# An attention and mixture-of-experts block on one Trainium2 core: one key tile fewer summed by matmuls in the long query blocks, and the last normalisation of a group moved from VectorE to ScalarE

## The chip, the core and the metric

The kernel runs on one core of one Trainium2 chip. The core has TensorE (PE in the rows), VectorE (DVE), ScalarE (ACT), GpSimd (POOL) and the engine that issues most DMAs (SP). Each has its own instruction queue and goes through it in order; semaphores tie the queues together. The metric is the device time of one execution in microseconds (us), and less is better. Between fast executions of one kernel it agrees within about 0.3%.

## The reference

Two sequences of 2048 tokens with 512 features go through one layer. All 16 heads have a dimension of 32 and share one key head and one value head.

```python
qkv = jnp.einsum('bsd,ed->bse', x, Wqkv_w) + Wqkv_b          # 512 for q, 32 for k, 32 for v
scores = jnp.einsum('bqhd,bkd->bhqk', q, k) * scale          # 16 heads, one k
scores = jnp.where(causal[None, None], scores, min_val)
attn = jax.nn.softmax(scores, axis=-1)
ctx = jnp.einsum('bhqk,bkd->bqhd', attn, v)
out = jnp.einsum('bsd,ed->bse', ctx, out_w) + out_b
...
x = _layernorm(x + attention(x))                             # x1
x = _layernorm(x + experts(x))                               # top 2 of 8 experts, bf16 matmuls
```

The layer normalisations have no gain and no bias: `(x - mean) / sqrt(var + 1e-5)` over the 512 features of a token.

## The kernel before, in words

A loop runs over the two sequences (`b`). In each, four **groups** `g` of 512 queries follow one another, and a group has four **blocks** `q` of 128 queries. Block `q` sees `q + 1` key tiles of 128 keys, the diagonal one first. So group 0 has 10 tiles, group 1 has 26, group 2 has 42 and group 3 has 58. `t` numbers the tiles of a sequence, `FIRST[q]` and `LAST[q]` are those of a block.

One tile goes through the engines as follows. TensorE writes its scores for all 16 heads in two halves of 1024 columns (`scores`, L1109, four matmuls of 512 columns), into a ring of three half buffers in PSUM. ScalarE takes the exponential of each half (`exp_tile`, L620) into one of six `prob` buffers. The diagonal tile is masked by GpSimd in two halves (`mask`, L492). TensorE multiplies by the values two tiles later (`times_values`, L1131, eight matmuls). A half of the ring is free again when its exponential is done: the second half of the scores of tile t + 1 waits for the first exponential of tile t.

The denominators are sums over keys. VectorE adds the `prob` buffers of a block into `psum_k` (`add`, L793, 128x2048 and both inputs in SBUF), one instruction a tile. The last `BY_PE[q]` tiles of a block are not added: in `denominators` TensorE sums them by matmuls with `ones` (L1149, eight for a tile), together with `psum_k`. `denominators(q)` comes four tiles after the block's last one, and waits for the block's last add. VectorE then inverts the sum and scales the context (L842 to L852).

After the attention tiles of a group come the output projection, the projections of the next group, x1, the router and the experts. The last piece of a group, `finish_experts(g)`, is put off on both TensorE and VectorE until the next group's attention has begun: TensorE issues the scores of the first tile and then the rest of the down projection (L1264), and VectorE adds each 128x512 result to `res`, takes mean and variance into `mv` (L866 to L870), and tells GpSimd by `mv_ready`. GpSimd makes `rstd` in two tiny instructions of 128x4 (`make_rstd`: L517 adds epsilon, L519 raises to the power -0.5). VectorE waits for that and scales four tiles of `res` (`normalise`, L876, `out_ready`). Only behind that stand its adds of the new group. The SP queue stores `res` as each tile's `out_ready` comes.

The order on each engine is the order of the code; there is no scheduler. `mv` and `rstd` exist once, and serve both normalisations of a group.

Of the kernel before, what the change touches and what calls it, by code (L numbers as in the profile page):

```python
# [35 lines left out]
P = 128  # L36
# [6 lines left out]
NG = S // BT  # L43
DC = D // P
TB = BT // P
# [16 lines left out]
LAST = [FIRST[q] + q for q in range(NQ)]  # L62
NT = len(TILES)

BY_PE = [0] + [1] * 9 + [2] * (NQ - 10)
ADDED = [t for q in range(NQ) for t in range(FIRST[q] + 1, LAST[q] + 1 - BY_PE[q])]
ADDS = len(ADDED)

# [61 lines left out]
def build(nc, xT, x, wqkvT, bq, bvk, owT, ob, rT, w1, w2, w3, out):  # L130
    ctx = ExitStack()
    with ctx:
# [51 lines left out]
        stats = sb("stats", [P, TB, 6])  # L184
        mv = sb("mv", [P, TB, 2])
        rstd = sb("rstd", [P, TB])
        rsc = sb("rsc", [P, TB, E])
        top8 = sb("top8", [P, TB, E])
        tidx = sb("tidx", [P, TB, E], U32)
# [32 lines left out]
        def half_of(t):  # L222
# [52 lines left out]
        mv_ready = sem("mv_ready")  # L275
        eps_in = sem("eps_in")
        rstd_ready = sem("rstd_ready")
        x1_ready = sem("x1_ready")
        x1_turned = sem("x1_turned")
        x1T_ready = sem("x1T_ready")  # L280
# [40 lines left out]
            xT_high: NG, xT_low: NG, part_done: NG, rpart_ready: NG,  # L321
            prod_done: E * NG,
            biased: 16 * NG, outproj: TB * NG, resid1: TB * NG, mv_ready: 2 * NG, eps_in: 2 * NG,
            rstd_ready: 2 * NG, x1_ready: TB * NG, x1_turned: TB * NG, x1T_ready: TB * NG,
            x1Tb_ready: TB * NG, routed: NG, dtop_ready: NG, etop_ready: NG, ghl_ready: NG,
            gates_turned: NG, gT_ready: NG, up_done: E * NG, gate_done: E * NG,
            silu_done: E * NG, h_done: E * NG, down_done: TB * NG, resid2: TB * NG,
# [110 lines left out]
        @block.gpsimd  # L438
        def _(pool):
            steps = [0]  # L440

            def step(ins):

                steps[0] += 1
                ins.then_inc(const_step, 1)
                pool.wait_ge(const_step, steps[0])

            nc.gpsimd.memset(rT_sb[:, :, :], 0.0).then_inc(rT_cleared, 1)
            step(nc.gpsimd.memset(ident[:, :], 0.0))
            step(nc.gpsimd.affine_select(out=ident[:, :], in_=ident[:, :], compare_op=ALU.not_equal, fill=1.0,  # L450
                                         base=0, pattern=[[-1, P]], channel_multiplier=1))
            step(nc.gpsimd.memset(pick_f, 0.0))
            for off in (0, E, 2 * E):
                step(nc.gpsimd.affine_select(out=pick_f, in_=pick_f, compare_op=ALU.not_equal,
                                             fill=1.0, base=-off, pattern=[[-1, E]],
                                             channel_multiplier=1))
            step(nc.gpsimd.memset(ident_b[:, :], 0.0))
            step(nc.gpsimd.affine_select(out=ident_b[:, :], in_=ident_b[:, :], compare_op=ALU.not_equal, fill=1.0,
                                         base=0, pattern=[[-1, P]], channel_multiplier=1))
            for e in range(E):  # L460
                step(nc.gpsimd.memset(iota8[:, e:e + 1], float(e)))
            step(nc.gpsimd.memset(ones[:, :], 1.0))
            step(nc.gpsimd.memset(ones_b[:, :], 1.0))

            step(nc.gpsimd.memset(head_pick[:, :], 1.0))
            step(nc.gpsimd.affine_select(out=head_pick[:, :], in_=head_pick[:, :], compare_op=ALU.is_ge, fill=0.0,
                                         base=0, pattern=[[-HD, HC]], channel_multiplier=1))
            step(nc.gpsimd.affine_select(out=head_pick[:, :], in_=head_pick[:, :], compare_op=ALU.is_ge, fill=0.0,
                                         base=HD - 1, pattern=[[HD, HC]], channel_multiplier=-1))
            step(nc.gpsimd.memset(causal_min[:, :], 3e38))  # L470
            step(nc.gpsimd.affine_select(out=causal_min[:, :], in_=causal_min[:, :], compare_op=ALU.is_ge,
                                         fill=-3e38, base=0, pattern=[[-1, P]], channel_multiplier=1))
            step(nc.gpsimd.memset(mhalf[:, :], -0.5))
            step(nc.gpsimd.memset(ghl[:, :, :], 0.0))
            step(nc.gpsimd.memset(fold_sel[:, :], 0.0))
            for c in range(HC):
                step(nc.gpsimd.affine_select(out=fold_sel[:, :], in_=fold_sel[:, :], compare_op=ALU.not_equal,
                                             fill=1.0, base=-c * HD, pattern=[[-1, E]], channel_multiplier=1))
            nc.gpsimd.memset(rden[:, :], 0.0).then_inc(consts_ready, 1)

            pool.wait_ge(weights_in, 3 * 16)
            pool.wait_ge(ow_low, 1)

            with pool.Fori(0, B) as b:
                def mask(q):

                    t = FIRST[q]
                    for half in range(2):
                        pool.wait_ge(exped, count(b, exped, 2 * t + half + 1))
                        pool.sem_inc(waited_apart, 1)  # L490
                        tile = prob[t % NP][:, half * HW:(half + 1) * HW].rearrange("p (h q) -> p h q", h=H // 2)
                        nc.gpsimd.affine_select(out=tile, in_=tile, compare_op=ALU.is_ge, fill=0.0, base=0,  # L492
                                                pattern=[[0, H // 2], [1, P]], channel_multiplier=-1).then_inc(masked, 1)

                def load_experts(part):

                    with pool.If(b < B - 1):
                        if part < 2:
                            dst, src = ((w1_sb, w1), (w3_sb, w3))[part]
                            for c in range(DC):  # L500
                                pool.dma_start(dst[:, :, c, :], src[:, c * P:(c + 1) * P, :]
                                               .rearrange("e p f -> p e f")).then_inc(experts_in, 16)
                        else:
                            pool.dma_start(w2_sb[:, :, :], w2.rearrange("e f d -> f e d")).then_inc(experts_in, 16)

                def add_bias(g):
                    pool.wait_ge(res_in[g % 2], count(b, res_in[g % 2], 16 * (g // 2 + 1)))
                    pool.sem_inc(waited_apart, 1)
                    pool.dma_start(res[g % 2][:, :, :],
                                   ob_sb[:, :].rearrange("p (t d) -> p t d", t=1).broadcast_to([P, TB, D]),  # L510
                                   accum_op=ALU.add).then_inc(biased, 16)

                def make_rstd(n):

                    pool.wait_ge(mv_ready, count(b, mv_ready, n))
                    pool.sem_inc(waited_apart, 1)
                    nc.gpsimd.tensor_scalar(rstd[:, :], mv[:, :, 1], EPS, None, ALU.add).then_inc(eps_in, 1)  # L517
                    pool.wait_ge(eps_in, count(b, eps_in, n))
                    nc.gpsimd.tensor_tensor(out=rstd[:, :], in0=rstd[:, :], in1=mhalf[:, :],  # L519
                                            op=ALU.pow).then_inc(rstd_ready, 1)  # L520

                for g in range(NG):
                    for q in range(TB * g, TB * (g + 1)):
                        mask(q)
                        if q == TB * g and g:
                            make_rstd(2 * g)
                        if q == TB * g + 1:
                            add_bias(g)
                        if q == 2:
                            load_experts(0)  # L530
                        if q == 3:
                            load_experts(1)
                            load_experts(2)
                    with if_more(pool, b, g):

                        pool.wait_ge(xT_high, count(b, xT_high, g + 1))
                        nc.gpsimd.tensor_tensor(out=xT_lo, in0=xT_raw[(g + 1) % 2],  # L537
                                                in1=xT_hi.bitcast(F32), op=ALU.subtract).then_inc(xT_low, 1)
                    make_rstd(2 * g + 1)
                make_rstd(2 * NG)  # L540

        @block.scalar
        def _(act):
# [62 lines left out]
            with act.Fori(0, B) as b:  # L606
# [17 lines left out]
                def split_high_context(g, t):  # L624
# [6 lines left out]
                    toks = slice(t * P, (t + 1) * P)  # L631
                    nc.scalar.activation(ctx_hi[:, t // 2, :, half_of(t)], ctxn[:, :, toks], ACT.Copy).then_inc(ctx_high, 1)  # L632

                def split_high_x(g):

                    act.wait_ge(xT_in, count(b, xT_in, 16 * g))
# [21 lines left out]
                for g in range(NG):  # L658
                    t1 = LAST[TB * g + TB - 1]
                    for t in range(FIRST[TB * g], t1 + 1):  # L660
                        exp_tile(t)
                        for n in range(TB - 1):
                            if split_at(TB * g + n, HIGH_LAG) == t:
                                split_high_context(g, n)
# [21 lines left out]
        def _(dve):  # L686
# [84 lines left out]
            with dve.Fori(0, B) as b:  # L771
# [106 lines left out]

                def finish_attention(g):

                    for t in range(TB):
                        if t == 3:
                            with if_more(dve, b, g):
# [75 lines left out]
                def finish_experts(g):  # L959
# [1 line left out]
                        dve.wait_ge(down_done, count(b, down_done, TB * g + t + 1))  # L961
                        last = residual(g, t, down_bank(g, t), resid2)
                    last.then_inc(mv_ready, 1)
                    normalise(g, 2 * g + 2, out_ready)

                for g in range(NG):
                    guard(g)
# [380 lines left out]
```

## Time and profile before

| | us |
|---|---|
| median of 3 runs (lowest, highest) | 1142.77 (1138.89, 1143.15) |
| the profiled execution, its own time | 1142.1 |
| its span, first to last instruction | 1140.3 |
| TensorE busy | 1085.1 (95%) |
| VectorE busy | 881.0 (77%) |
| ScalarE busy | 715.3 (63%) |
| GpSimd busy | 192.4 (17%) |
| mean granted TensorE clock | 0.985 of full speed |

Busy shares are means over stages with different limits. In the attention stage of the later groups all of TensorE, VectorE and ScalarE are nearly full, so it is the stage, and in it the order of waits, that must be read. A matmul's end is modelled, so the distance from one start to the next tells more than its duration.

### The profile page before, as it was taken

What the parts mean: (1) busy time and instruction counts of PE and PEld (TensorE: products, weight loads), DVE (VectorE), ACT (ScalarE), POOL (GpSimd) and SP (SyncE); (2) the same over time, 40 slices, a digit from 0 to 9 for tenths busy, and PEclk for the clock granted to TensorE, in tenths of its full rate; (3) what the DMA queues carried; (4) which work ended last, traced back from release to release, by engine and by line L of the source; (5) the groups of instructions that cost most, each with busy time, mean ns of one, the idle gap of its engine ahead of it and who ended that gap; (6) DMA issues with size and microseconds to landing.
All of it is one profiled execution on the core that took longest, in us unless ns stands there. A gap on an engine that the chain in (4) does not pass through costs nothing.

```text
span 1140.3 us, 18344 instructions
## 1 busy us (share of the span) xinstructions
PE 1085.1 (95%) x6080; PEld 521.2 (46%) x6080; DVE 881.0 (77%) x1103; ACT 715.3 (63%) x844; POOL 192.4 (17%) x156
## 2 busy tenths in 40 slices
PE   6699999999999999999989999999999999999986
PEld 4246434743336543334734743474333654333442
DVE  3176799679985688988676669976998668898856
ACT  5344676558883488886436458744888437888721
POOL 2250223012112012111013013210211201211000
PEclk9799999999999999999999999999999999999988
DMA  4893430253001622000163254016400152200000
GB/s 139 220 168 77 117 74 9 72 126 92 1 1 39 149 75 38 1 1 18 46 153 86 65 121 112 2 40 146 112 1 1 39 119 68 38 1 1 2 1 37
DMA packets 41101, 74.36 MB, mean 65 GB/s; under 512 B 14224, under 2 KB 15248, under 8 KB 40976
## 3 DMA queue, kind: packets, MB, share of 16 engines
q1 hardware_dynamic: 25392, 58.74, 19.6%
q0 software_dynamic: 13584, 11.54, 6.8%
q10 hardware_dynamic: 2000, 2.51, 0.7%
q8 instruction: 67, 1.10, 0.4%
q14 instruction: 58, 0.48, 0.1%
HBM read 25.58 MB, written 8.39 MB: 30 GB/s over the span
## 4 chain that ended last, share of the span: by engine, by line
PE 83%; DVE 7%; issue 4%; ACT 2%; SPq 2%; POOL 2%; ACTq 0%; DMA 0%; DVEq 0%; POOLq 0%
PE sc L1109 22%; PE bank L1131 20%; PE sc L996 10%; PE sc L1249 9%; PE bank L996 7%; PE sc L1149 3%; DVE psum_k L793 3%; PE sc L1264 2%; SPq L393 2%; PE bank L1149 2%; PE bank L1264 2%; PE sc L1197 1%; PE bank L1257 1%; POOL prob L492 1%; ACT prob L620 1%
## 5 line engine op out<-in xcount | busy, mean ns | idle before, releaser
L620 ACT ACTIVATE prob<-sc 128x1024 f32<-128x1024 f32 x544 | 525.6, 1025 | 144.9 <-PE sc L1109 144.7
L793 DVE TENSOR_TENSOR psum_k<-psum_k,prob 128x2048 f32<-128x2048 f32 x170 | 403.5, 2373 | 4.7
L1109 PE MATMUL sc<-q_st,k_st 128*128 128x512 f32 x1088 | 329.4, 424 | 20.0 <-DMA q_st<-q_lo 8.7
L1109 PEld LDWEIGHTS sc<-q_st,k_st 128*128 128x128 f32 x1088 | 184.6, 189 | 262.9 <-ACT prob L620 177.7
L1131 PE MATMUL bank<-prob,v_sb 128*32 128x512 f32 x2176 | 287.4, 606 | 0.6 <-POOL prob L492 0.5
L492 POOL TENSOR_SCALAR_AFFINE_SELECT prob<-prob 128x1024 f32<-128x1024 f32 x64 | 112.2, 1793 | 539.8 <-ACT prob L620 539.8
L1249 PE MATMUL sc<-prob,w_sb 128*128 128x512 bf16 x512 | 120.8, 382 | 0.0
L1131 PEld LDWEIGHTS bank<-prob,v_sb 128*32 128x32 f32 x2176 | 44.4, 108 | 104.9 <-issue 87.4
L650 ACT ACTIVATE prob<-sc 128x512 f32<-128x512 f32 x64 | 38.0, 594 | 76.0 <-PE sc L1249 76.0
L996 PE MATMUL bank<-q_st,wq_hi 128*128 128x512 f32 x240 | 80.7, 401 | 0.0
L793 DVE TENSOR_TENSOR psum_k<-prob 128x2048 f32<-128x2048 f32 x28 | 64.0, 2287 | 19.8 <-POOL prob L492 15.8
L1249 PEld LDWEIGHTS sc<-prob,w_sb 128*128 128x128 bf16 x512 | 49.8, 100 | 63.8 <-issue 9.2
L632 ACT ACTIVATE q_hi<-ctxn 128x512 fp32r<-128x512 f32 x32 | 20.2, 632 | 64.2 <-DVE ctxn L852 64.2
L537 POOL TENSOR_TENSOR q_st<-res,q_st 128x2048 fp32r<-128x2048 f32 x7 | 35.4, 5050 | 126.2 <-ACT q_st L637 126.1
L907 DVE TENSOR_TENSOR prob<-sc,prob 128x512 f32<-128x512 f32 x64 | 43.5, 680 | 15.1 <-ACT prob L650 14.9
L996 PE MATMUL sc<-ow_hi,q_hi 128*128 128x512 f32 x128 | 52.3, 409 | 0.0
L954 DVE TENSOR_TENSOR psum_k<-bank,prob 128x512 bf16<-128x512 f32 x64 | 42.4, 683 | 11.1 <-PE bank L1257 10.4
L996 PE MATMUL sc<-ow_lo,q_hi 128*128 128x512 f32 x128 | 50.6, 395 | 0.0
L996 PE MATMUL sc<-ow_hi,q_lo 128*128 128x512 f32 x128 | 50.6, 395 | 0.0
L996 PEld LDWEIGHTS bank<-q_st,wq_hi 128*128 128x128 f32 x240 | 45.4, 189 | 10.2 <-issue 0.4
L580 ACT ACTIVATE q_hi<-bank,bq_sb 128x512 fp32r<-128x512 f32 x30 | 20.6, 688 | 46.0 <-PE bank L996 46.0
L866 DVE TENSOR_TENSOR res<-sc,res 128x512 f32<-128x512 f32 x48 | 32.3, 673 | 20.3 <-PE sc L1264 13.2
(138 smaller groups left out, 996.0 us busy)
## 6 DMA issues: line engine op xcount, KB each, us to landing
q_st<-q_hi SPq DMA_DIRECT2D x128, 128.0 KB, 2.4
q_st<-q_lo SPq DMA_DIRECT2D x128, 128.0 KB, 2.4
res<-in_x SPq DMA_DIRECT2D x8, 1024.0 KB, 5.1
res<-ob_sb POOLq DMA_DIRECT2D x8, 1024.0 KB, 8.7
out_x<-res SPq DMA_DIRECT2D x32, 256.0 KB, 2.2
res<-in_xT SPq DMA_DIRECT2D x7, 1024.0 KB, 5.3
w_sb<-in_w POOLq DMA_DIRECT2D x8, 256.0 KB, 8.6
prob<-in_wqkvT ACTq DMA_DIRECT2D x4, 288.0 KB, 6.1
```

Of the source, the lines that this page charges most:

```text
L492: nc.gpsimd.affine_select(out=tile, in_=tile, compare_op=ALU.is_ge, fill=0.0, base=0, pattern=[[0, H // 2], [1, P]], channel_multiplier=-1 ...
L620: nc.scalar.activation(prob[t % NP][:, half * HW:(half + 1) * HW], score_half(q // TB, 2 * t + half).rearrange("p m n -> p (m n)"), ACT.Ex ...
L650: nc.scalar.activation(silu[e % 4], LOW[2 * (e % 3)], ACT.Silu).then_inc(silu_done, 1)
L793: nc.vector.tensor_tensor(acc[:, :], first[:, :], prob[t % NP][:, :], ALU.add).then_inc(add_v, 1)
L907: nc.vector.tensor_tensor(prod[e % 4], LOW[2 * (e % 3) + 1], silu[e % 4], ALU.mult).then_inc(prod_done, 1)
L954: nc.vector.tensor_tensor(hT[:, e, :], gate_bank(e)[:, :], prod[e % 4], ALU.mult).then_inc(h_done, 1)
L996: last = nc.tensor.matmul(dst, stationary[i][:, c, cols], moving[j][:, c, :], start=(c == 0 and n == 0), stop=(c == DC - 1 and n == 2))
L1109: last = nc.tensor.matmul(dst, k_st[:, k * P:(k + 1) * P], q_st[slot][:, c * HJ:(c + 1) * HJ, at:at + P], start=True, stop=not shift)
L1131: last = nc.tensor.matmul(top[q % 2][c * HD:(c + 1) * HD, :], v_sb[:, k, :], prob[t % NP][:, c * BT:(c + 1) * BT], start=(t == PV_ORDER[FI ...
L1149: last = nc.tensor.matmul(den_bank(q)[c * HD:(c + 1) * HD, :], ones[:, :], src[:, c * BT:(c + 1) * BT], start=(n == 0), stop=(n == len(par ...
L1249: last = nc.tensor.matmul(LOW[2 * (e % 3) + n], w[:, e, c, :], x1Tb[:, c, :], start=(c == 0), stop=(c == DC - 1))
L1264: last = nc.tensor.matmul(down_bank(g, t), hT[:, e, t * P:(t + 1) * P], w2_sb[:, e, :], start=(e == 0), stop=(e == E - 1))
```

## The change

Two things change. `BY_PE` was 2 for blocks 10 to 15 and is now 1, so each of these blocks has one more add on VectorE and one tile fewer in `denominators`: 6 in a sequence, 12 in all. And for all groups but the last of a sequence, the normalisation behind the experts leaves VectorE. GpSimd now makes `nmr = -mean * rstd` as well, in two more tiny instructions, and ScalarE applies it as `res * rstd + nmr`, one 128x512 instruction behind each of the exponentials of tiles 4, 5, 6 and 7 of the next group (`OUT_LAG`). That happens in 6 of the 8 groups.

```diff
-BY_PE = [0] + [1] * 9 + [2] * (NQ - 10)
+BY_PE = [0] + [1] * (NQ - 1)
+OUT_LAG = 4
...
+        nmr = sb("nmr", [P, TB])
...
+                def make_nmr(g):
+
+                    pool.wait_ge(rstd_ready, count(b, rstd_ready, 2 * g + 2))
+                    pool.sem_inc(waited_apart, 1)
+                    nc.gpsimd.tensor_scalar(nmr[:, :], mv[:, :, 0], -1.0, None, ALU.mult).then_inc(nmean_ready, 1)
+                    pool.wait_ge(nmean_ready, count(b, nmean_ready, g + 1))
+                    pool.sem_inc(waited_apart, 1)
+                    nc.gpsimd.tensor_tensor(out=nmr[:, :], in0=nmr[:, :], in1=rstd[:, :],
+                                            op=ALU.mult).then_inc(nmr_ready, 1)
+
                 for g in range(NG):
                     for q in range(TB * g, TB * (g + 1)):
                         mask(q)
                         if q == TB * g and g:
                             make_rstd(2 * g)
+                            make_nmr(g - 1)
...
+                    if g:
+                        pool.wait_ge(out_ready, count(b, out_ready, TB * g))
+                        pool.sem_inc(waited_apart, 1)
                     make_rstd(2 * g + 1)
...
+                def normalise_out(g, t):
+                    act.wait_ge(nmr_ready, count(b, nmr_ready, g + 1))
+                    r = res[g % 2][:, t, :]
+                    nc.scalar.activation(r, r, ACT.Identity, bias=nmr[:, t:t + 1],
+                                         scale=rstd[:, t:t + 1]).then_inc(out_ready, 1)
+
...
                     for t in range(FIRST[TB * g], t1 + 1):
                         exp_tile(t)
+                        if g and OUT_LAG <= t - FIRST[TB * g] < OUT_LAG + TB:
+                            normalise_out(g - 1, t - FIRST[TB * g] - OUT_LAG)
...
                 def finish_attention(g):
 
+                    if g:
+                        dve.wait_ge(nmr_ready, count(b, nmr_ready, g))
                     for t in range(TB):
...
                     last.then_inc(mv_ready, 1)
-                    normalise(g, 2 * g + 2, out_ready)
+                    if g == NG - 1:
+                        normalise(g, 2 * g + 2, out_ready)
```

On VectorE, at the start of a group (here the second group of a sequence), the queue of before goes from the last statistics through the wait for `rstd_ready` to the first adds:

```order
L870 BN_AGGR mv<-stats 128x2 [waits v_step]
L873 REGISTER_ALU
L876 TENSOR_SCALAR res<-res,mv,rstd 128x512 [waits rstd_ready]
L876 TENSOR_SCALAR res<-res,mv,rstd 128x512 x3
L785 REGISTER_ALU
L788 REGISTER_ALU [waits exped]
L793 TENSOR_TENSOR psum_k<-prob 128x2048 [waits summed,masked]
```

and in the changed kernel:

```order
L896 BN_AGGR mv<-stats 128x2 [waits v_step]
L811 REGISTER_ALU
L814 REGISTER_ALU [waits exped]
L819 TENSOR_TENSOR psum_k<-prob 128x2048 [waits summed,masked]
L811 REGISTER_ALU
L818 REGISTER_ALU [waits exped]
L819 TENSOR_TENSOR psum_k<-psum_k,prob 128x2048 [waits add_v]
```

The wait and the four instructions behind it are gone, and the adds follow the statistics at once.

On GpSimd, at the same place, the queue between the masks of the group's first and second block was:

```order
L492 AFFINE_SELECT prob<-prob 128x1024 [waits exped]
L515 REGISTER_ALU
L517 TENSOR_SCALAR rstd<-mv 128x4 [waits mv_ready]
L519 TENSOR_TENSOR rstd<-rstd,mhalf 128x4 [waits eps_in]
L489 REGISTER_ALU
L492 AFFINE_SELECT prob<-prob 128x1024 [waits exped]
```

and is now:

```order
L496 AFFINE_SELECT prob<-prob 128x1024 [waits exped]
L519 REGISTER_ALU
L521 TENSOR_SCALAR rstd<-mv 128x4 [waits mv_ready]
L523 TENSOR_TENSOR rstd<-rstd,mhalf 128x4 [waits eps_in]
L530 TENSOR_SCALAR nmr<-mv 128x4 [waits rstd_ready]
L531 ISA
L533 TENSOR_TENSOR nmr<-nmr,rstd 128x4 [waits nmean_ready]
L493 REGISTER_ALU
L496 AFFINE_SELECT prob<-prob 128x1024 [waits exped]
```

Two tiny instructions are added to the chain, each of the four waiting for the one ahead of it.

On ScalarE, behind the exponentials of tile 4 of the group (again the second group), the changed kernel has:

```order
L638 ACTIVATE prob<-sc 128x1024 [waits scored]
L653 ISA
L655 ACTIVATE res<-res,nmr,rstd 128x512 [waits nmr_ready]
L628 REGISTER_ALU
L637 REGISTER_ALU [waits summed,pv_done]
L638 ACTIVATE prob<-sc 128x1024 [waits scored]
```

Before, one exponential followed the other there; now a wait for GpSimd's last tiny instruction stands between them. No load of an activation table was added anywhere in the queue.

## Rows read from the trace of the kernel before

**Rows 1.** Page, busy us of each engine (share of the span), instructions.

```profile
PE 1085.1 (95%) x6080; PEld 521.2 (46%) x6080; DVE 881.0 (77%) x1103; ACT 715.3 (63%) x844; POOL 192.4 (17%) x156
```

**Rows 2.** Page, groups: line, engine, operation, shapes, count | busy us, mean ns | idle before, releaser.

```profile
L620 ACT ACTIVATE prob<-sc 128x1024 f32<-128x1024 f32 x544 | 525.6, 1025 | 144.9 <-PE sc L1109 144.7
L793 DVE TENSOR_TENSOR psum_k<-psum_k,prob 128x2048 f32<-128x2048 f32 x170 | 403.5, 2373 | 4.7
...
L632 ACT ACTIVATE q_hi<-ctxn 128x512 fp32r<-128x512 f32 x32 | 20.2, 632 | 64.2 <-DVE ctxn L852 64.2
...
L580 ACT ACTIVATE q_hi<-bank,bq_sb 128x512 fp32r<-128x512 f32 x30 | 20.6, 688 | 46.0 <-PE bank L996 46.0
```

**Rows 3.** Timeline, start of group 3, first sequence: start us, length us, what.

```profile
403.19 7.57 ACT L620 ACTIVATE prob<-sc 128x1024 f32<-128x1024 f32 x8 [3.87 <-PE sc L1109]
...
406.44 0.18 DVE L870 BATCH_NORM_AGGREGATE mv<-stats 128x2 f32<-128x6 f32 x1
406.82 0.22 POOL L517 TENSOR_SCALAR rstd<-mv 128x4 f32<-128x4 f32 x1 [6.11 <-DVE mv L870]
...
407.13 1.03 POOL L519 TENSOR_TENSOR rstd<-rstd,mhalf 128x4 f32<-128x4 f32 x1
...
408.20 1.92 DVE L876 TENSOR_SCALAR res<-res,mv,rstd 128x512 f32<-128x512 f32 x4 [1.57 <-POOL rstd L519]
...
410.03 2.28 DVE L793 TENSOR_TENSOR psum_k<-prob 128x2048 f32<-128x2048 f32 x1
...
410.17 1.19 PE L1109 MATMUL sc<-q_st,k_st 128*128 128x512 f32 x4
410.94 1.94 ACT L620 ACTIVATE prob<-sc 128x1024 f32<-128x1024 f32 x2 [0.18 <-PE sc L1109]
...
412.29 1.19 PE L1109 MATMUL sc<-q_st,k_st 128*128 128x512 f32 x4
```

**Rows 4.** Timeline, start of group 1, first sequence.

```profile
130.72 7.58 ACT L620 ACTIVATE prob<-sc 128x1024 f32<-128x1024 f32 x8 [4.16 <-PE sc L1109]
...
133.98 0.18 DVE L870 BATCH_NORM_AGGREGATE mv<-stats 128x2 f32<-128x6 f32 x1
```

**Rows 5.** Two lines of GpSimd, 128x8 each: ns shortest/median/longest, first and last start us.

```profile
L454 POOL TENSOR_SCALAR_AFFINE_SELECT prob<-prob x3: 192/193/193, 2.0 to 2.7; 128x8 f32<-128x8 f32 x3
...
L477 POOL TENSOR_SCALAR_AFFINE_SELECT fold_sel<-fold_sel x4: 461/540/698, 7.2 to 9.2; 128x8 f32<-128x8 f32 x4
```

**Rows 6.** Timeline of the preamble from 7 us.

```profile
7.23 2.67 POOL L477 TENSOR_SCALAR_AFFINE_SELECT fold_sel<-fold_sel 128x8 f32<-128x8 f32 x4
...
8.32 0.68 DVE L692 TENSOR_TENSOR q_st<-res,q_st 128x512 fp32r<-128x512 f32 x1
```

**Rows 7.** GpSimd's masks and VectorE's adds by line, in short stretches: ns shortest/median/longest.

```profile
L492 POOL TENSOR_SCALAR_AFFINE_SELECT prob<-prob x2: 1091/1094/1097, 398.6 to 399.6; 128x1024 f32<-128x1024 f32 x2
...
L492 POOL TENSOR_SCALAR_AFFINE_SELECT prob<-prob x2: 2783/2958/3132, 429.1 to 431.8; 128x1024 f32<-128x1024 f32 x2
...
L793 DVE TENSOR_TENSOR psum_k<-psum_k,prob x2: 2294/2676/3058, 428.6 to 431.0; 128x2048 f32<-128x2048 f32 x2
```

**Rows 8.** Timeline of PE, the denominators of block 12.

```profile
435.91 1.90 PE L1149 MATMUL sc<-prob,ones 128*32 128x512 f32 x16
437.62 1.04 PE L1149 MATMUL sc<-psum_k,ones 128*32 128x512 f32 x8
```

**Rows 9.** Waits of PE: who for whom, us in total, times, longest us.

```profile
PE sc L1109 <- DVE rden L842: 3.1, 4, 1.0
```

**Rows 10.** Stretches: busy us of PE, PEld, DVE, ACT, POOL (instructions), granted PE clock, DMA share, GB/s.

```profile
48.90:52.10 3.20, 3.20 (x17) 0.60 (x16) 0.00 (x0) 1.02 (x1) 0.00 (x0) 0.50 0.99 369
...
1093.40:1096.60 3.20, 0.00 (x0) 0.00 (x0) 1.80 (x5) 0.00 (x0) 0.71 (x2) 1.00 0.00 0
1096.80:1097.70 0.90, 0.00 (x0) 0.00 (x0) 0.50 (x2) 0.00 (x0) 0.36 (x1) 0.50 0.00 0
```

**Rows 11.** Timeline of DVE, blocks 14 and 15, first sequence.

```profile
499.46 2.29 DVE L793 TENSOR_TENSOR psum_k<-prob 128x2048 f32<-128x2048 f32 x1 [2.03 <-POOL prob L492]
...
538.32 0.72 DVE L842 STREAM_TRANSPOSE rden<-bank 128x512 f32<-128x512 f32 x1 [4.37 <-PE bank L1149]
```

More of the change, by code:

```diff
@@ L277, in build @@
         rstd_ready = sem("rstd_ready")
+        nmean_ready = sem("nmean_ready")
+        nmr_ready = sem("nmr_ready")
         x1_ready = sem("x1_ready")
@@ L323, in build @@
             biased: 16 * NG, outproj: TB * NG, resid1: TB * NG, mv_ready: 2 * NG, eps_in: 2 * NG,
-            rstd_ready: 2 * NG, x1_ready: TB * NG, x1_turned: TB * NG, x1T_ready: TB * NG,
+            rstd_ready: 2 * NG, nmean_ready: NG - 1, nmr_ready: NG - 1, x1_ready: TB * NG, x1_turned: TB * NG, x1T_ready: TB * NG,
             x1Tb_ready: TB * NG, routed: NG, dtop_ready: NG, etop_ready: NG, ghl_ready: NG,
```

## The prediction

> **What bounds the kernel now.** I read the page first. TensorE is busy for 95% of the span, VectorE for 77%, ScalarE for 63% [rows 1]; a tile that leaves TensorE should be worth its time, if the others keep up. The groups say how near they are: an exponential of half a tile takes 1.025 us, an add 2.29 us and 2.37 in the mean [rows 2, 7]. Then I read the timeline at the start of a group, where the change puts its new wait.
>
> In the steady attention stage TensorE starts the scores of a tile every 2.12 us (410.17, 412.29) [rows 3]. ScalarE does eight exponentials back to back in 7.57 us, so 1.89 us a tile, and waits only 0.18 us for scores [rows 3]. VectorE needs 2.3 us for a tile's add. So three engines run within 10% of each other, and TensorE sets the pace because two or three tiles of a block are not added.
>
> At the start of group 3 VectorE finishes the statistics at 406.62 (406.44 + 0.18). Call this moment E. GpSimd makes rstd until 408.16, E + 1.5; VectorE waits 1.57 us for it, scales for 1.9 us and starts its adds at 410.03, E + 3.4 [rows 3]. ScalarE meanwhile has gone through the exponentials of tiles 1 to 4 by 410.76, E + 4.1. In group 1 the same distance is 138.30 - 134.16 = 4.1 us [rows 4].
>
> **The change, part by part.**
>
> *Denominators.* In block 12 two tiles by matmul start at 435.91 and psum_k's own eight at 437.62, so one tile is 1.71 / 2 = 0.86 us of TensorE, without a gap [rows 8]. Twelve tiles go: -10.3 us, all on the path.
>
> *VectorE.* It gains 12 adds x 2.29 = 27.5 us and loses 6 x (1.57 + 1.9) = 20.8 us of waiting and scaling. TensorE waited for VectorE's inverses 3.1 us in all, in groups where VectorE ran late behind that scaling [rows 9]; adds that start 3.4 us earlier give this back: -3.1 us.
>
> *ScalarE's four instructions a group.* The trace has no scaling of 128x512 with two per-partition operands here. A plain copy of that size takes 632 ns, one with a per-partition bias 688 ns [rows 2]. At full pace an instruction costs less than its length (exponentials of 1.025 us come every 0.946 us, 0.08 less) [rows 2, 3], so I take 0.688 - 0.08, rounded to 0.6 us. The bounds are 0.55 (the copy) and 0.69. A tile with one then costs ScalarE 1.89 + 0.6 = 2.49 us against TensorE's 2.12: 0.37 us late each. If ScalarE enters with slack the first two are hidden; if it enters late, three are paid, 1.1 us. The Trainium skill (ScalarE: Activation LUTs, What ACT_TABLE_LOAD costs) gives a pointer operand 93 ns each and 93 ns of overlap between instructions. By that page the scaling would cost about 0.71 us, and three tiles 1.4 us instead of 1.1, 2 us more over the six groups.
>
> *The chain on GpSimd, which decides.* ScalarE now needs nmr at E + 4.1. Undisturbed, the chain is ready well before: rstd at E + 1.5, then two tiny instructions of 0.22 us with about 0.1 us between, so E + 2.3. But before, VectorE stood still while GpSimd made rstd. Now it goes straight into its adds, and a row shows what such instructions do to GpSimd. In the preamble tiny selects of 128x8 take 0.19 us alone, and 0.46 to 0.70 us while VectorE runs subtractions with both inputs in SBUF, 0.68 us each [rows 5, 6]: four take 2.67 us, one for each subtraction. The masks agree: 1.09 us alone, 2.8 and 3.1 us under adds, and the add between them takes 3.06 instead of 2.29 us [rows 7]. So a GpSimd instruction waits for the add that runs, finishes shortly behind it, and by the time its successor comes the next add is running. The Trainium skill (SBUF — State Buffer, SBUF: two separate sides) states this as a rule: GpSimd shares a pair of ports with VectorE, exclusively and for a whole instruction, and an instruction of VectorE with two SBUF inputs blocks one of GpSimd that reads SBUF. By that rule all four tiny instructions pay an add each; the trace of before shows it for 128x8 and 128x1024, not for 128x4.
>
> Step by step. Add 1 starts at about E + 0.1: only two register instructions stand ahead of it, and its tiles' exponentials are done. GpSimd's first instruction starts at E + 0.2 (406.82) [rows 3], so narrowly behind. It ends with add 1 at E + 2.5. The power (1.03 us) waits for add 2 (E + 4.8) and ends at about E + 5.7, holding add 3 back by 0.8, as the masks do, to E + 7.8. The third ends there, the fourth behind add 4 at E + 10.2. Tiles 1 to 4 have their exponentials, so all four adds can run while ScalarE stands. ScalarE, ready at E + 4.1, waits 6 us.
>
> *What TensorE pays.* Its scores of tile 6 start at 412.29, and their second half (0.56 later, E + 6.2) needs the first exponential of tile 5. That is now done at E + 10.2 + 0.1 + 0.6 + 1.0 = E + 11.9: TensorE stands 5.7 us, and then pays 1.1 us for the three later scalings. Nothing later gives this back, since TensorE has no other gaps in these stages: 6.8 us a group, 40.8 us in six.
>
> *The clock.* TensorE stood from about 1093.3; in the stretch to 1096.60 the granted clock was still 1.00 (2.4 GHz), in 1096.80 to 1097.70 it was 0.50 (1.2 GHz) [rows 10]. A stand of 5.7 us is longer than that, so the clock should fall. Back at work, 48.90 to 52.10 was a stretch of 3.2 us of full work at 0.50 [rows 10]. That costs half, 1.6 us, of which about 0.6 is hidden by ScalarE's lag: 1.0 us a group, +6 us; bounds 0 and 10.
>
> Sum for the profiled execution: 1142.1 - 10.3 - 3.1 + 40.8 + 6 = 1175.5. The median of the runs is 0.7 above the profiled one. The tiny instructions might hold the ports for less than their length (the 0.8 behind the power, 6 x 0.8 = 4.8 us, is the part that I trust least), so I round down to 1173.
>
> **The rivals.**
>
> *One add fewer (28%).* If GpSimd's first instruction slips in ahead of add 1, it ends at E + 0.4, and the chain pays three adds: nmr at about E + 8.2. That is only 0.1 us of order between two engines. For it: the first instruction started 0.2 us behind E, and add 1 has two waits to go through. TensorE then stands 3.7 us and pays 1.1: 28.8 us in six groups; the clock may hold. 1142.1 - 13.4 + 28.8 = 1157.5; with the clock's fall up to 1163.
>
> *The chain is not held up: faster (15%).* If instructions of four elements get through between or beside the adds, nmr is there at E + 2.3 and ScalarE never waits for it. It turns at E + 4.1: one blocked instruction is still harmless, two are not. Then ScalarE's lag costs 2 x 0.37 = 0.7 us a group, 4.4 in all. VectorE becomes nearly the bound in group 3: 4 more adds are 9.2 us, it starts 3.4 earlier, and TensorE leaves 2.6 us sooner. It had 4.37 us idle ahead of the last inverse, of which about 2.6 are that sum's own matmuls, and five shorter pauses of 6.9 us in all, of which the longest is 2.03 [rows 11]. So 8.4 us against 8.7: between 0 and 3 us late, 1.5 twice. 1142.1 - 13.4 + 4.4 + 3 = 1136. Against it: rows 5 to 7.
>
> *The clock stays low (5%).* If it stays at 1.2 GHz for some 8 us of attention in each group, as after a poorly filled stretch, the forecast grows by 6 x 3 = 18 us, to 1191.
>
> **How the numbers follow.** The forecast's own case has 48%, the rest (4%) I leave to effects that I don't see, half of them near no change. The likeliest time is 1173. To hold 8 in 10 the range has to take in the case of three adds, from 1150 (its price without the third scaling's lag and with the ports held shorter) to 1184 (the upper clock bound and scalings of 0.69 us): 1150 to 1184. The likeliest case's own range is 1165 to 1184. A difference under 0.5%, 5.7 us, is about what a measurement of this kernel can't tell from none. Faster than that: the third case, and only most of it, 0.13; within it 0.05; slower 0.82.
>
> **What would show it.** Right: in the six groups the four tiny GpSimd instructions span 8 to 10 us, each ending just behind an add; ScalarE has an idle time of 4 to 6 us ahead of its first scaling, put down to GpSimd; TensorE has six gaps of 3.5 to 6 us in its scores, and its clock falls to 0.50 behind them; the denominators of blocks 10 to 15 are 16 matmuls; VectorE has more idle time later in the groups. Wrong: tiny instructions of 0.2 us beside running adds, and no such idle time. Then VectorE's last add of blocks 13 to 15 would be what TensorE's denominators wait for. If only the number of adds paid is off, the step that fails is the order at E.

## The result, and the profile after

The changed kernel takes 1203.34 us (median of 4 runs, 1202.23 to 1204.59), beside 1142.15 us for the kernel before: a ratio of 1.0543, interval 1.0521 to 1.0566. That is 61 us slower, twice the 31 us that the forecast added, and above the range. The profiled execution took 1202.23 us, its span is 1200.1 us.

The page: busy us by engine, then three groups (mean ns behind the busy time). They answer to [rows 1, 2].

```profile
PE 1095.5 (91%) x5960; PEld 524.5 (44%) x5984; DVE 905.9 (75%) x1091; ACT 730.1 (61%) x868; POOL 229.1 (19%) x168
...
L819 DVE TENSOR_TENSOR psum_k<-psum_k,prob 128x2048 f32<-128x2048 f32 x182 | 440.9, 2422 | 18.9 <-ACT prob L638 14.3
...
L1138 PE MATMUL sc<-q_st,k_st 128*128 128x512 f32 x1088 | 338.0, 432 | 47.8 <-ACT prob L638 25.5
...
L521 POOL TENSOR_SCALAR rstd<-mv 128x4 f32<-128x4 f32 x16 | 15.9, 992 | 270.3 <-DVE mv L896 270.3
```

TensorE's share of busy time fell from 95% to 91%. GpSimd's instruction of four elements a partition now takes 992 ns in the mean, where it took 224 to 229.

The timeline at the start of group 3, first sequence, which answers to [rows 3]:

```profile
424.49 0.18 DVE L896 BATCH_NORM_AGGREGATE mv<-stats 128x2 f32<-128x6 f32 x1
424.76 2.29 DVE L819 TENSOR_TENSOR psum_k<-prob 128x2048 f32<-128x2048 f32 x1
424.86 2.27 POOL L521 TENSOR_SCALAR rstd<-mv 128x4 f32<-128x4 f32 x1 [6.43 <-DVE mv L896]
...
427.08 6.95 DVE L819 TENSOR_TENSOR psum_k<-psum_k,prob 128x2048 f32<-128x2048 f32 x3
427.22 3.05 POOL L523 TENSOR_TENSOR rstd<-rstd,mhalf 128x4 f32<-128x4 f32 x1
...
430.46 1.33 POOL L530 TENSOR_SCALAR nmr<-mv 128x4 f32<-128x4 f32 x1 [0.20 <-POOL rstd L523]
431.98 2.11 POOL L533 TENSOR_TENSOR nmr<-nmr,rstd 128x4 f32<-128x4 f32 x1 [0.18 <-POOL nmr L530]
434.12 0.81 ACT L655 ACTIVATE res<-res,nmr,rstd 128x512 f32<-128x512 f32 x1 [5.30 <-POOL nmr L533]
...
435.89 0.96 PE L1138 MATMUL sc<-q_st,k_st 128*128 128x512 f32 x2 [4.81 <-ACT prob L638]
...
436.88 2.29 DVE L819 TENSOR_TENSOR psum_k<-psum_k,prob 128x2048 f32<-128x2048 f32 x1 [2.85 <-ACT prob L638]
```

Read it down the column of ends. Add 1 ends at 427.05 and GpSimd's first instruction at 427.13. The power ends 0.9 us behind add 2, the third instruction with add 3, the fourth (434.09) just behind add 4 (434.03). Each link of the chain costs one add. ScalarE stands 5.30 us, TensorE 4.81 us, and VectorE then runs out of exponentials as well.

The waits of the whole execution, in total us, times and longest:

```profile
ACT res L655 <- POOL nmr L533: 27.3, 6, 5.3
...
PE sc L1138 <- ACT prob L638: 25.5, 12, 4.8
...
PE bank L1178 <- DVE psum_k L819: 19.7, 4, 6.4
```

The last row was not forecast: TensorE waits 19.7 us for VectorE's last add, ahead of the last denominators of groups 2 and 3. The end of group 3 on the timeline:

```profile
553.06 13.62 DVE L819 TENSOR_TENSOR psum_k<-psum_k,prob 128x2048 f32<-128x2048 f32 x4
...
556.08 1.92 ACT L661 ACTIVATE q_st<-res 128x2048 fp32r<-128x2048 f32 x1
...
558.08 6.45 POOL L552 TENSOR_TENSOR q_st<-res,q_st 128x2048 fp32r<-128x2048 f32 x1 [31.14 <-ACT q_st L661]
...
566.81 1.94 PE L1178 MATMUL bank<-prob,ones 128*32 128x512 f32 x8 [6.41 <-DVE psum_k L819]
```

and the chain in the same stretch:

```profile
557.72 2.30 DVE psum_k L819
...
560.04 6.64 DVE psum_k L819
```

The same place in the kernel before:

```profile
524.67 9.27 DVE L793 TENSOR_TENSOR psum_k<-psum_k,prob 128x2048 f32<-128x2048 f32 x4
...
533.15 5.32 POOL L537 TENSOR_TENSOR q_st<-res,q_st 128x2048 fp32r<-128x2048 f32 x1 [33.72 <-ACT q_st L637]
```

GpSimd splits the next group's inputs there, with one 128x2048 subtraction that follows ScalarE's last instruction of the group. It waits for the add that runs (to 560.02), and then the last add waits for it: 6.64 us instead of 2.3. Before, the subtraction came at 533.15, during VectorE's last add of the group, and VectorE was idle from 533.94 (524.67 + 9.27). The one extra add of the block fell behind it. The last group of the kernel has no subtraction behind it, and there TensorE waits 2.1 us, the shortest of the four.

The stretches show the granted clock (columns as in [rows 10]):

```profile
431.10:435.80 4.70, 0.00 (x0) 0.00 (x0) 2.90 (x2) 1.68 (x3) 2.80 (x2) 1.00 0.00 0
436.00:439.50 3.50, 3.50 (x12) 1.15 (x13) 2.39 (x2) 3.50 (x5) 0.00 (x0) 0.53 0.40 152
...
562.60:566.70 4.10, 0.00 (x0) 0.00 (x0) 4.08 (x1) 0.00 (x0) 1.93 (x1) 0.50 0.03 11
566.90:572.70 5.80, 5.80 (x22) 2.37 (x23) 1.93 (x4) 0.00 (x0) 0.00 (x0) 0.50 0.43 167
573.00:576.00 3.00, 3.00 (x15) 2.40 (x14) 2.14 (x4) 2.12 (x3) 0.00 (x0) 1.00 0.00 0
```

TensorE stood in the first and third stretch, and worked in the second and fourth at about 1.2 GHz.

Where the 59.8 us of span went, from the starts of matmuls on both timelines (first scores, last scores and the first matmul of the last denominators of each group; in group 3, first sequence, from first to last scores it was 132.8 us before and is 140.0):

| part of the two sequences | us |
|---|---|
| first to last scores, the six groups with a moved normalisation | +34.8 |
| last scores to the first matmul of the last denominators, groups 2 and 3, both sequences | +19.8 |
| from there to the next group or the end, the same four (a tile of matmuls fewer in each) | +4.8 |
| the rest (preamble, groups 0, tails of groups 1) | +0.4 |

### The profile page after: what moved, and what is told of

The parts are those of the page before. It is cut to its first block, busy times and chain, and to the rows that moved or that the text cites. A ratio compares the mean times of both kernels' runs of the same rounds, so it can differ in the third digit from the quotient of the medians.

```text
span 1200.1 us, 18218 instructions
## 1 busy us (share of the span) xinstructions
PE 1095.5 (91%) x5960; PEld 524.5 (44%) x5984; DVE 905.9 (75%) x1091; ACT 730.1 (61%) x868; POOL 229.1 (19%) x168
## 4 chain that ended last, share of the span: by engine, by line
PE 66%; DVE 16%; issue 7%; POOL 6%; ACT 2%; SPq 2%; ACTq 0%; DVEq 0%; DMA 0%; POOLq 0%
PE sc L1138 16%; PE bank L1160 14%; DVE psum_k L819 10%; PE sc L1278 9%; PE sc L1025 9%; PE bank L1025 7%; PE sc L1293 2%; PE sc L1178 2%; DVE stats L895 2%; POOL prob L496 2%; PE bank L1178 2%; POOL rstd L523 2%; DVE res L892 2%; SPq L397 2%; ACT prob L638 2%
## 5 line engine op out<-in xcount | busy, mean ns | idle before, releaser
L819 DVE TENSOR_TENSOR psum_k<-psum_k,prob 128x2048 f32<-128x2048 f32 x182 | 440.9, 2422 | 18.9 <-ACT prob L638 14.3
L1138 PE MATMUL sc<-q_st,k_st 128*128 128x512 f32 x1088 | 338.0, 432 | 47.8 <-ACT prob L638 25.5
L1138 PEld LDWEIGHTS sc<-q_st,k_st 128*128 128x128 f32 x1088 | 188.3, 193 | 299.5 <-ACT prob L638 203.4
L1160 PE MATMUL bank<-prob,v_sb 128*32 128x512 f32 x2176 | 292.8, 616 | 1.7 <-POOL prob L496 1.5
L496 POOL TENSOR_SCALAR_AFFINE_SELECT prob<-prob 128x1024 f32<-128x1024 f32 x64 | 104.0, 1657 | 551.6 <-ACT prob L638 551.6
L1278 PE MATMUL sc<-prob,w_sb 128*128 128x512 bf16 x488 | 117.7, 381 | 2.3 <-issue 1.4
L819 DVE TENSOR_TENSOR psum_k<-prob 128x2048 f32<-128x2048 f32 x28 | 64.1, 2289 | 38.8 <-ACT prob L638 31.3
L521 POOL TENSOR_SCALAR rstd<-mv 128x4 f32<-128x4 f32 x16 | 15.9, 992 | 270.3 <-DVE mv L896 270.3
L552 POOL TENSOR_TENSOR q_st<-res,q_st 128x2048 fp32r<-128x2048 f32 x7 | 38.4, 5488 | 118.7 <-ACT q_st L661 118.6
L868 DVE STREAM_TRANSPOSE rden<-sc 128x512 f32<-128x512 f32 x24 | 17.1, 713 | 48.9 <-PE sc L1178 48.9
```

The source lines that it names most:

```text
L819: nc.vector.tensor_tensor(acc[:, :], first[:, :], prob[t % NP][:, :], ALU.add).then_inc(add_v, 1)
L1138: last = nc.tensor.matmul(dst, k_st[:, k * P:(k + 1) * P], q_st[slot][:, c * HJ:(c + 1) * HJ, at:at + P], start=True, stop=not shift)
L1160: last = nc.tensor.matmul(top[q % 2][c * HD:(c + 1) * HD, :], v_sb[:, k, :], prob[t % NP][:, c * BT:(c + 1) * BT], start=(t == PV_ORDER[FI ...
L1278: last = nc.tensor.matmul(LOW[2 * (e % 3) + n], w[:, e, c, :], x1Tb[:, c, :], start=(c == 0), stop=(c == DC - 1))
```

## The experiments

Each is the changed kernel with the edit shown, unless it says otherwise. The two theories ahead of them: the start of a group costs what it does because each link of GpSimd's chain waits for an add, and its end because the last add waits for GpSimd's subtraction, and these are separate; against it, that one late chain makes VectorE late up to the end of the group, or that VectorE has simply too much to do.

### The move alone

```diff
-BY_PE = [0] + [1] * (NQ - 1)
+BY_PE = [0] + [1] * 9 + [2] * (NQ - 10)
```

> The changed kernel with BY_PE as before: only the move of the normalisation. Theory (two separate costs: the blocked GpSimd chain at a group's start, and a last add of groups 2 and 3 that runs into GpSimd's 128x2048 subtraction): the three gaps of TensorE of 4.6 to 4.8 us and two of 2.6 us at the starts stay, and the 5.6 and 6.4 us gaps ahead of a group's last denominators go, since VectorE's last add is one tile earlier. 1178 to 1188 us. Rival (the late start of a group is what makes the adds late, so the chain causes both): the gaps ahead of the last denominators stay at 4 us or more, 1200 us or more.

1181.29 us, ratio 1.0348 (1.0327 to 1.0368). Its waits:

```profile
ACT res L655 <- POOL nmr L533: 28.1, 6, 5.3
PE sc L1138 <- ACT prob L638: 26.2, 12, 4.8
```

No wait for an add ahead of the last denominators is left. So the chain, which is all there, doesn't cause the tail.

### The tiles alone

The kernel before, with the new `BY_PE`.

```diff
-BY_PE = [0] + [1] * 9 + [2] * (NQ - 10)
+BY_PE = [0] + [1] * (NQ - 1)
```

> The kernel before with BY_PE of 1 throughout: only the tiles. Theory: no chain, so no gap at tile 6 of a group; the last add of groups 2 and 3 still meets the subtraction, and VectorE, which starts its adds 3.4 us later here, makes TensorE wait inside group 3 too. Gaps ahead of the last denominators of 5.5 us or more in three places, about 20 us in all, some 5 us for the lower clock behind them, -7 us of matmuls, a few us of waits in group 3: 1160 to 1172 us. Rival (the tail exists only because of the late start): 1130 to 1137 us, no gap over 2 us there.

1170.03 us, ratio 1.0248 (1.0229 to 1.0266). Its waits:

```profile
PE bank L1149 <- DVE psum_k L793: 19.5, 4, 6.4
PE sc L1109 <- DVE rden L842: 6.6, 10, 1.0
```

The wait for the last adds is there in full without the move, and the waits for VectorE's inverses rose from 3.1 us [rows 9] to 6.6. One tile of matmuls fewer in a block makes the kernel slower by itself. The two halves add up to 38.8 + 27.6 = 66 us against 61 together.

### VectorE waits for the chain

```diff
                     if g == NG - 1:
                         normalise(g, 2 * g + 2, out_ready)
+                    else:
+                        dve.wait_ge(nmr_ready, count(b, nmr_ready, g + 1))
+                        dve.sem_inc(waited_apart, 1)
```

> The changed kernel, and VectorE waits for nmr before its first add of a group, so that no add runs beside the four tiny GpSimd instructions. Theory of the shared port: each tiny instruction is back at its length alone (0.2 and 1.0 us), nmr is ready 2.3 us behind the statistics, ScalarE doesn't wait for it, and the gaps at tile 6 go; the tail stays and grows a little since the adds start 2.4 us later. 1160 to 1175 us. Rival (the instructions are slow for another reason, such as ScalarE's or TensorE's traffic): their lengths stay, 1200 us or more.

1172.04 us, ratio 1.0251 (1.0224 to 1.0279). The last two links by line (ns shortest/median/longest), first in this kernel:

```profile
L530 POOL TENSOR_SCALAR nmr<-mv x6: 243/247/249, 137.1 to 981.7; 128x4 f32<-128x4 f32 x6
L533 POOL TENSOR_TENSOR nmr<-nmr,rstd x6: 198/199/203, 137.6 to 982.1; 128x4 f32<-128x4 f32 x6
```

and in the changed kernel:

```profile
L530 POOL TENSOR_SCALAR nmr<-mv x6: 1322/1326/1333, 139.7 to 1009.9; 128x4 f32<-128x4 f32 x6
L533 POOL TENSOR_TENSOR nmr<-nmr,rstd x6: 199/2107/2109, 141.2 to 1011.4; 128x4 f32<-128x4 f32 x6
```

With no add beside them the same instructions take a fifth and a tenth of the time, and ScalarE no longer waits for `nmr` (VectorE does, by this edit). This is the rule of the Trainium skill (SBUF — State Buffer, SBUF: two separate sides): VectorE with two SBUF inputs and GpSimd, when it reads SBUF, take a shared pair of ports, and one of them holds it for a whole instruction. The runs agree, now for four elements too, with one exception: the power runs its last 0.9 us beside add 3 and doesn't hold it back (427.08 6.95 for three adds). There the measurement decides.

Other stretches tell that it isn't just any work of VectorE. Beside GpSimd's 128x2048 subtraction in the changed kernel, a product with one input in PSUM and one in SBUF keeps its 0.69 us, and the subtraction takes 4.65 us:

```profile
657.19 4.65 POOL L552 TENSOR_TENSOR q_st<-res,q_st 128x2048 fp32r<-128x2048 f32 x1 [11.06 <-ACT q_st L661]
...
660.84 0.69 DVE L878 TENSOR_TENSOR ctxn<-bank,rden 128x512 f32<-128x512 f32 x1
```

while in the kernel before, at the end of group 1, a 128x512 subtraction of VectorE with both inputs in SBUF, 0.68 us elsewhere, takes 5.15 us beside it:

```profile
191.12 5.70 POOL L537 TENSOR_TENSOR q_st<-res,q_st 128x2048 fp32r<-128x2048 f32 x1 [15.55 <-ACT q_st L637]
192.21 5.15 DVE L861 TENSOR_TENSOR q_lo<-ctxn,q_hi 128x512 fp32r<-128x512 f32 x1
```

That what is held are ports no run shows by itself: no add with one SBUF input was tried in the place of the others.

### ScalarE asks later

```diff
-OUT_LAG = 4
+OUT_LAG = 8
```

> The changed kernel with OUT_LAG 8 instead of 4: ScalarE asks for nmr 8.5 us later, when the blocked chain is done anyway. Theory: the tiny instructions stay as long as in the changed kernel (2.3, 3.0, 1.3, up to 2.1 us) but nobody waits; the gaps at tile 6 go, the tail stays. 1160 to 1170 us. Rival (the scalings themselves, not the wait, load ScalarE so that TensorE starves): gaps move to tiles 9 to 12 with the same total, 1195 us or more.

1165.94 us, ratio 1.021 (1.0192 to 1.0228). Its waits:

```profile
PE bank L1178 <- DVE psum_k L819: 19.7, 4, 6.4
PE sc L1138 <- DVE rden L868: 5.6, 8, 1.0
```

The links are as long as before (in the run with the old counts below too), and nobody waits for them. The start of the groups was a matter of when `nmr` is asked for, 37 us of it. ScalarE's four instructions aren't free, though: where they stand in group 3, TensorE starts a tile every 2.53 us instead of 2.12, twice:

```profile
430.34 1.60 PE L1138 MATMUL sc<-q_st,k_st 128*128 128x512 f32 x4
...
432.87 1.61 PE L1138 MATMUL sc<-q_st,k_st 128*128 128x512 f32 x4
```

With the 0.08 us of the tile ahead of them that makes 0.9 us in a group 3, far from the 30 us and more of the rival.

### One link fewer

VectorE writes `-mean` into `nmr` ahead of `mv_ready`, and GpSimd has three tiny instructions instead of four.

```diff
-                    nc.gpsimd.tensor_scalar(nmr[:, :], mv[:, :, 0], -1.0, None, ALU.mult).then_inc(nmean_ready, 1)
...
-                    last.then_inc(mv_ready, 1)
+                    if g == NG - 1:
+                        last.then_inc(mv_ready, 1)
+                    else:
+                        step(last)
+                        nc.vector.tensor_scalar(nmr[:, :], mv[:, :, 0], -1.0, None, ALU.mult).then_inc(mv_ready, 1)
```

> The changed kernel with one link fewer in the chain: VectorE writes -mean itself, in one 128x4 instruction ahead of mv_ready, so GpSimd has three tiny instructions. Theory (each link is held until a running add ends): in groups 2 and 3 nmr is ready 1.8 to 2.3 us earlier and TensorE's gap at tile 6 falls from 4.8 to 2.5 to 3 us; in group 1, where VectorE has only three adds to do, by 0.3 us or less. Perhaps the clock holds behind the shorter gaps. 1188 to 1196 us in all. Rival (a fixed delay of the chain, whatever its links): 1201 us or more.

1190.96 us, ratio 1.0436 (1.04 to 1.0473).

```profile
ACT res L651 <- POOL nmr L529: 19.7, 6, 3.3
...
PE sc L1138 <- ACT prob L634: 18.1, 13, 2.8
```

ScalarE's longest wait fell by 2.0 us, from 5.3 to 3.3, TensorE's from 4.8 to 2.8. One link is worth nearly one add of 2.3 us where VectorE has adds to do. In group 1, where the last link ran free anyway, TensorE's stand didn't shrink (2.81 us in the first sequence, 2.65 in the changed kernel).

### The subtraction behind the last add

```diff
                         pool.wait_ge(xT_high, count(b, xT_high, g + 1))
+                        pool.sem_inc(waited_apart, 1)
+                        pool.wait_ge(add_v, count(b, add_v, adds_until(LAST[TB * g + TB - 1])))
+                        pool.sem_inc(waited_apart, 1)
```

> The changed kernel, and GpSimd's 128x2048 subtraction at a group's end also waits for the group's last add, so it can't run ahead of it. Theory (the tail is a last add blocked by that subtraction): the last add is back at 2.3 us, the gaps of 5.6 and 6.4 us ahead of the last denominators fall to about 1.5 to 2 us as in the last group, where there is no such subtraction, and the lower clock behind them goes; the gaps at tile 6 stay. About 3 x 4 us and 3 to 5 us of clock less than 1203: 1184 to 1190 us. Rival (VectorE is simply late by its extra adds): the gaps stay, or the projections wait for the later split, 1200 us or more.

1180.09 us, ratio 1.0337 (1.0316 to 1.0359), 23 us under the changed kernel. The end of group 3 on its timeline:

```profile
546.83 6.95 DVE L822 TENSOR_TENSOR psum_k<-psum_k,prob 128x2048 f32<-128x2048 f32 x3
...
553.90 1.90 PE L1181 MATMUL bank<-prob,ones 128*32 128x512 f32 x8 [2.07 <-DVE psum_k L822]
553.96 4.60 POOL L555 TENSOR_TENSOR q_st<-res,q_st 128x2048 fp32r<-128x2048 f32 x1 [35.58 <-DVE psum_k L822]
```

Three adds take 6.95 us again, TensorE waits 2.07 instead of 6.41, and the wait for adds fell to 6.7 us in all. It came out 4 us below what I expected: the four waits shrank by 13 us, and the stretches behind them, up to the next group or the end, by 7 us, on which I had put 3 to 5. The clock did not stay up everywhere: in 554.00 to 557.30, behind the wait of 2.07 us, it was 0.50. The 1.3 us (group 2) and 2.1 us (group 3) of wait that are left are plain lateness of VectorE.

### Both cures, the extra adds kept

`OUT_LAG` 8 and the wait of the run above.

> OUT_LAG 8, BY_PE of 1 throughout, and GpSimd's subtraction held behind the group's last add: both costs taken out, the extra adds kept. Theory: against OUT_LAG 8 alone (1166 us) the tail falls from 19.8 to about 7 us and its clock with it, as in the run with the split behind the last add alone, which was 23 us faster than the changed kernel: 1143 to 1150 us, with waits of TensorE for VectorE of 2 to 4 us left in each group 3. Rival (the two cures overlap, the later split then delays the projections): 1155 us or more.

1147.1 us, ratio 1.0051 (1.0031 to 1.0071). What is left:

```profile
PE bank L1181 <- DVE psum_k L822: 6.7, 4, 2.1
PE sc L1141 <- DVE rden L871: 5.6, 8, 1.0
```

TensorE waits 12.3 us for VectorE, 8.5 more than the kernel before (3.1 and 0.7), which takes most of the 10.3 us of matmuls saved. ScalarE's four instructions cost their part as with `OUT_LAG` 8 alone.

### Later, and the last block of a group keeps two

```diff
-BY_PE = [0] + [1] * (NQ - 1)
-OUT_LAG = 4
+BY_PE = [0] + [1 + (q > 10 and q % TB == TB - 1) for q in range(1, NQ)]
+OUT_LAG = 8
```

> OUT_LAG 8 and BY_PE 1 except in blocks 11 and 15, the last of their groups, which keep 2. Theory: neither cost is left, no gap at tile 6 and none ahead of the last denominators; against the run with OUT_LAG 8 alone 20 us of gaps and 4 us of clock go and 4 x 0.86 us of matmuls come back. 1141 to 1147 us, so no better than before, because 8 fewer tiles of matmuls (7 us) are spent on waits for VectorE in group 3. Rival (VectorE's total load is what costs, wherever its adds stand): 1155 us or more.

1148.64 us, ratio 1.0058 (1.004 to 1.0076): 2 us above the range. Both large costs are gone. TensorE's waits for VectorE's inverses are 5.6 us as above. Two gaps of 1.5 and 2.1 us, one in each sequence, stand inside the last denominators of group 3, where I expected none. They aren't lateness of VectorE: its last add ended at 535.34, the first six of these matmuls ran from 535.62, and only then comes the gap, which the profile puts down to nothing. Its cause stays open.

### Later, with the old counts

`OUT_LAG` 8 and the old `BY_PE`: the move alone, without its wait.

> OUT_LAG 8 and the old BY_PE: the normalisation alone moved, asked for late enough. Theory: the chain is blocked as in the changed kernel and nobody waits for it; VectorE starts its adds 3.4 us earlier, and TensorE's few waits for it (3 us in all) go: 1136 to 1143 us. Rival (ScalarE's extra 0.8 us instructions starve TensorE): 1148 us or more.

1145.93 us, ratio 1.0027 (1.0014 to 1.0041): 3 us above the range. In both sequences VectorE pauses at the start of group 3, and TensorE waits 1.7 and 1.8 us:

```profile
401.39 0.69 DVE L895 BATCH_NORM_STATS2 stats<-res 128x6 f32<-128x512 f32 x1 [1.79 <-issue]
...
403.13 1.63 PE L1138 MATMUL sc<-q_st,k_st 128*128 128x512 f32 x6 [1.67 <-DVE res L892]
```

The pause waits for nothing that the profile shows. It stands also in the first run, which has the same code but for the lag, and TensorE's gap with it, and not in the runs with other counts. That VectorE waits there for its own code is a rival that no run tests: 8 KB of instructions begin to load within 0.15 us ahead of each of the four pauses (399.45 here), but also at the same place in the changed kernel (418.64), which has no pause. Why the pause is there stays open.

Without these 3.5 us the move is worth nothing either way. TensorE's waits for the inverses fell only from 3.1 to 2.1 us, where I expected them to go. By the starts of matmuls, tiles with a scaling cost about 4 us in the six groups, and VectorE's earlier adds give about 3 back.

### Later, with two early extra tiles

```diff
-BY_PE = [0] + [1] * (NQ - 1)
-OUT_LAG = 4
+BY_PE = [0] + [1] * 10 + [2, 1, 2, 2, 2]
+OUT_LAG = 8
```

> OUT_LAG 8 and BY_PE 1 up to block 10 and in block 12, else 2: only the extra adds that stand early in their group, where the 3.4 us that VectorE gains pay for them. Theory: 4 tiles of matmuls fewer, 3.4 us, no new wait in group 3 and none at the tails: 1139 to 1143 us, at best 3 us faster than before. Rival (any add beyond the old count makes TensorE wait for VectorE in group 3 by as much as it saves): 1145 us or more, as with 11 and 15 kept at 2.

1141.28 us beside 1141.73, ratio 0.9997 (0.9985 to 1.0009).

```profile
PE sc L1138 <- DVE rden L868: 2.8, 4, 1.0
```

No new wait, 4 tiles of matmuls fewer (3.4 us), and no gain that can be measured: by the interval it is under 1.7 us. The tiles with a scaling take their 2.53 us here too. Nothing tried here beats the kernel before.

## Why the prediction was wrong, point by point

**The direction and the chain were right.** The first instruction lost the race to add 1 by 0.1 us (424.76 against 424.86), as forecast, and the chain paid four adds in groups 2 and 3. `nmr` came at 434.09, 9.4 us behind the statistics (424.67), where I had 10.2: the power does not hold the next add back, so the 0.8 us that I trusted least was not there. TensorE stood 4.8 us instead of 5.7. In group 1 only three adds are there before the next one needs a mask; the last link ran free in 0.2 us (the shortest L533), and TensorE stood 2.65 us. I had looked at group 1 only for the distance of 4.1 us.

**The scaling was under-priced, and it hardly mattered.** It takes 0.81 us, where my upper bound was 0.69, the length with one per-partition operand; the next exponential starts 0.72 us behind its start (434.12, 434.84), where I had 0.6. The 93 ns that the Trainium skill (ScalarE: Activation LUTs, What ACT_TABLE_LOAD costs) gives for each pointer operand were the better guide. Still, with `OUT_LAG` 8 a tile with a scaling takes 2.53 us, and I had 2.49.

**The term of -3.1 us was not there.** TensorE's waits for the inverses rose to 6.6 us instead of going. They did not come mainly from the scaling that left VectorE: with the move alone and no wait for it they were still 2.1 us. From first to last scores the six groups cost +34.8 us, and the forecast's terms for the same stretch give 40.8 + 6 - 3.1 - 8 x 0.86 = 36.8. That the two are near is luck. The tiles 6 and 7 of the groups, where stand, scalings and clock fall, cost 36.6 us, where the forecast had 46.8; the inverses cost 3.5 us more instead of 3.1 less.

**The clock was right in kind.** It fell to 0.50 behind the stands of 4.8 us and those of 5.6 and 6.4 us, and also behind the 2.1 us at the kernel's last denominators. Of the two stands of 2.6 us in group 1, one was followed by 0.50 (142.80 to 146.00) and the other by 1.00 (724.70 to 728.00). Group 3's tail ran 5.8 us of work at the lower clock, and the stage behind it is 2.7 us longer.

**The step that failed is the one on VectorE.** It gained 12 adds, and the sum has no term for them. Only in the third rival did I weigh them, 8.4 us of need in group 3 against 8.7 us of idle time, and came to 0 to 3 us. I used the idle time ahead of the last inverse of group 3 [rows 11] as room for an add. It was not free room: GpSimd's subtraction stands right behind ScalarE's last exponential, and an add that comes behind its start takes 6.64 us instead of 2.30. I had the rule, two rows that showed it, and that row of 4.37 us, and applied the rule only to the instructions that the change added, not to the adds that it moved. The kernel before even pays such a collision, with the 5.15 us at 192.21 shown above, and I had not read it. The tail cost 19.8 us, and the stretch behind it 4.8 us by the clock, where the forecast had -3.4 (4 x 0.86) for both. With these 28 us the sum of 1175.5 would have been 1203.5, beside 1202.2 for the profiled execution.

**The rival with the extra adds as a bound** had the right place and the wrong mechanism; so had the sign that I gave for it, denominators that wait for VectorE's last add. Its slower share is real as well: with the subtraction out of the way TensorE still waits 12.3 us for VectorE, 8.5 more than before. So even without collisions the 12 tiles bring nothing: 1147.1 us against 1141.7.

## What to carry to other kernels

When VectorE runs long instructions with two SBUF inputs back to back, count a chain on GpSimd in links times that instruction, not in its own nanoseconds, and ask for its result that much later. And when work is added to VectorE, find the long GpSimd instruction that follows the last of it: an instruction that slips behind the start of such a one can pay nearly its whole length (4.3 of 4.65 us here). Idle time of an engine is room only if what the added work shares is free then too.

## What the runs showed of the hardware that was not expected

- A power of 128x4 on GpSimd is held until a running add ends (3.05 us instead of 1.03), but does not hold the next add, which keeps its 2.29 us (427.08 6.95 x3). A mask of 128x1024 in the same place does: 3.06 us [rows 7].
- A ScalarE instruction of 128x512 with a per-partition bias and scale takes 0.81 us; with the bias alone, and its input in PSUM, it is 0.69 [rows 2].
- GpSimd's 128x2048 subtraction makes an add of VectorE take 6.64 us instead of 2.30, and leaves a product with one input in PSUM at 0.69 us.
- A pause of 1.6 to 1.8 us on VectorE between two instructions, put down to nothing, at one place in both sequences; and one of 1.5 and 2.1 us on TensorE in another run.
